# Third softmax's maxima: values' second half first, the queries' last two token tiles after maximum 7

## Chip, cores and metric

The kernel runs on 1 core of one Trainium2 chip. The metric is the device time of one execution in microseconds (us), as the median of several runs.

## What is computed

Input: 16 sequences (batches) of 1024 tokens with 256 channels. Each goes through a Nyström attention block and then through an adapter-gated feed-forward block, each with a LayerNorm before it, a LayerNorm on its output and a residual. Cut to what matters:

```python
def attention(x, w_qkv, w_proj):                   # 16 heads of 16 channels, 64 landmarks
    Q, K, V = split(x @ w_qkv)
    Q_l, K_l = Q.reshape(b, H, M, n // M, HD).mean(-2), K.reshape(b, H, M, n // M, HD).mean(-2)
    kernel1 = softmax(Q @ K_l.T)                   # 1024 x 64 per head
    kernel2 = softmax(Q_l @ K_l.T)                 # 64 x 64
    kernel3 = softmax(Q_l @ K.T)                   # 64 x 1024
    SV = (kernel1 @ iterative_inv(kernel2)) @ (kernel3 @ V)
    return SV @ w_proj

x = x + layernorm(attention(layernorm(x)))
x = x + layernorm(ffn(layernorm(x)))               # base product plus the adapter of the best expert of 8
```

The third softmax (kernel3) needs for each of its rows the maximum of the scores over all 1024 tokens before it can take exponentials.

## The kernel before, in words

The program is written engine by engine: `block.sync` (the DMA queue, SP), `block.gpsimd` (POOL), `block.scalar` (ACT), `block.tensor` (PE) and `block.vector` (DVE) each hold one list of steps per batch, in a function `body(b, more)`. Each engine executes its list strictly in the order in which it is written, and semaphores tie the lists together. The attention of batch b and the feed-forward part of batch b - 1 are interleaved in the same body, so batch 0 has no feed-forward steps, and batches 1 to 15 have them.

**The PSUM ring.** Attention products go through three PSUM banks in turn (`ringA`). The table `USES_A` lists all uses in the order of the TensorE list, and use n has bank n mod 3. `get(b, kind, k)` makes TensorE wait until the use three places earlier has been read. A use of kind `pk` (a token tile of the keys or queries, k from 0 to 7; 0 to 3 keys, 4 to 7 queries) is read twice: ACT copies it as its float16 high part (L634), then DVE subtracts that from it and stores the low part (L1467), and only then is the bank free. A use of kind `pv` (quarter of the value projection, k from 0 to 3) is read once, by ACT (L659). A use of kind `m3` (one product of maxima, k from 0 to 15) is read once, by DVE (L1518).

**The stage around the change.** After the keys, the landmarks and the values' first half come, on TensorE:

- token tiles 4 and 5 (L880), the scores of kernel2 (L972);
- products m3 0 to 3 (L1013), token tile 6, m3 4, token tile 7, m3 5 to 8, values 2, m3 9 to 12, values 3, m3 13 to 15;
- of the feed-forward part of batch b - 1: the channel sums (L1158), then the hidden layer's tile 0 (L1172), the transpose of the folded maxima (L1027), hidden tiles 1 to 3;
- the loop over k of 16: `maxima1` (L1022), `scores3` (L1046), `sum_values` (L1060) and more. `scores3(b, 0)` waits for `fold3`, a DMA.

**ACT** runs in that stage: `staged(2)` (token tiles 4 and 5), `halves2(0)`, `staged(3)` (tiles 6 and 7), `halves2(1)`, `values(2, 3)`. `halves2(g)` (L708) writes the float16 high part of half g of the normalised feed-forward input of batch b - 1. It waits for POOL, which normalises (`norm2`, L534), and POOL then waits for it: `x2lo` (L574) subtracts half g's high part. `staged(3)` also waits for the DMA copies out of the buffer that it overwrites (`stk[1]`).

**SP.** For each pair of token tiles, 12 copies move the staged parts into the stacked operands `KS` and `QS` (L429). Group j = 2 is tiles 4 and 5, group 3 is tiles 6 and 7. In the middle of group 2, after 6 of its 12 copies, stand the two DMA transposes of the feed-forward input (`transposes2`, L399). Each waits for POOL's `x2lo` of its half. After group 2's other 6 copies comes the fold of the third softmax's maxima (L405), which waits for F3T (L673), and then group 3:

```python
for q in range(4):
    if j == 2 and q == 2 and not first(b):
        transposes2(b - 1)
    for a, part in enumerate((0, 1, 0)):
        sp.dma_start(S[32 * a:32 * a + 32, 4 * (j % 2) + q, :],
                     stage[32 * q:32 * q + 32, j % 2, part, :]).then_inc(stk[j].sem, 16)
```

`maxima1(b, 0)` waits for all 12 copies of group 2, and `scores3(b, 0)` for the fold.

Of the kernel before, what the change touches and what calls it, by code (L numbers as in the profile page):

```python
# [40 lines left out]
def sandwich_kernel(nc, x, w_qkv, w_proj, W_base, b_base, Wd1, bd1, Wd2, bd2, Wa_down, ba_down, Wa_up, ba_up, out):  # L41
# [23 lines left out]
    with ctx:  # L65
# [3 lines left out]
        def sig(name, per_batch, unit=1):  # L69
# [102 lines left out]

        USES_A = ([("pk", k) for k in range(4)] + [("kl", 0), ("ql", 0)] + [("pv", k) for k in range(2)]
                  + [("lk", k) for k in range(3)] + [("lq", k) for k in range(2)] + [("pk", k) for k in (4, 5)]
                  + [("m3", k) for k in range(4)] + [("pk", 6), ("m3", 4), ("pk", 7)]
                  + [("m3", k) for k in range(5, 9)] + [("pv", 2)] + [("m3", k) for k in range(9, 13)] + [("pv", 3)]
                  + [("m3", k) for k in range(13, 16)] + [("f3", 0)])
        for k in range(16):
            USES_A += [("m1", k), ("s3", k)]
        USES_A += [("f1", 0)]  # L180
# [429 lines left out]
        def _(act):  # L610
# [17 lines left out]
            def staged(b, js):  # L628
                for j in js:
                    if j >= 2:  # L630
                        act.wait_ge(stk[j - 2].sem, stk[j - 2].at(b, 12))
                    for h in range(2):
                        k = 2 * j + h
                        A(stage[:, j % 2, 0, h * HALF:(h + 1) * HALF], take(b, "pk", k)[:, :], ACT.Copy)\  # L634
                            .then_inc(pk_hi.sem, 1)
# [21 lines left out]
            def values(b, ks):  # L657
                for k in ks:
                    A(V[:, 2 * k:2 * k + 2, :, :], take(b, "pv", k)[:, :].rearrange("p (t a d) -> p t a d", t=2, a=PAIRS),  # L659
                      ACT.Copy).then_inc(freed["pv"].sem, 1)  # L660
# [86 lines left out]
            def body(b, more):  # L747

                ffn = not first(b)
                staged(b, (0, 1))  # L750
                landmarks(b)
                values(b, (0, 1))
                landmark_stack(b)
                staged(b, (2,))
                if ffn:
                    halves2(b - 1, (0,))
                staged(b, (3,))
                if ffn:
                    halves2(b - 1, (1,))
                values(b, (2, 3))  # L760
                if ffn:
                    sums2(b - 1)
                    hidden(b - 1, 0)
                fold_rows3(b)
                kernel2_exp(b)
                if ffn:
                    for t in (1, 2, 3):
                        hidden(b - 1, t)
                for k in range(16):
                    exp3(b, k)  # L770
                    if k == 6:
                        kernel2_transposed(b)
                    if ffn and k in (1, 3, 5, 7):
                        hidden(b - 1, 4 + k // 2)
                fold_rows1(b)
                for k in range(5):
                    ns_copy(b, k)
                    if ffn and k == 4:
                        adapter(b - 1)
                    if first(b) and k == 0:  # L780
                        act.wait_ge(s_setpe.sem, 1)
                        for c in range(KC):
                            A(f_w2T[:, c, :, :], ringF[c][:, :].rearrange("p (q n) -> p q n", q=EP), ACT.Copy).then_inc(s_w2t.sem, 1)
                    if 1 <= k < 4:
                        exp1(b, 2 * k - 2)
                        exp1(b, 2 * k - 1)
                    if k == 3:
                        exp1(b, 6)
                        exp1(b, 7)
                    if more and k < 2:  # L790
                        halves1(b + 1, (k,))
                if ffn:
                    for k in range(4):
                        ffn_out(b - 1, k)
                if first(b):
                    ffn_reduction()
                for k in range(ESLOTS, 2 * ESLOTS):
                    exp1(b, k)
                attn_out(b, (0, 1))
                if more:  # L800
                    pooled(b + 1)
                attn_out(b, (2, 3))
# [18 lines left out]
        def _(pe):  # L821
# [122 lines left out]
            def values(b, ks):  # L944
                for k in ks:
                    ps = get(b, "pv", k)
                    for i in range(2):
                        t = 2 * k + i
                        ins = three(ps[:, i * C:(i + 1) * C], lambda a, kc: xT[:, t, a, kc, :],
                                    lambda a, kc: wqkv[:, a, kc, 2 * C:3 * C])  # L950
                    done(ins, "pv")
# [280 lines left out]
            def body(b, more):  # L1232

                ffn_too = not first(b)
                project(b)
                tokens(b, (4, 5))
                kernel2_scores(b)
                for k in range(4):
                    maxima3(b, k)
                tokens(b, (6,))  # L1240
                for k in range(4, 16):
                    maxima3(b, k)
                    if k == 4:
                        tokens(b, (7,))
                    if k in (8, 12):
                        values(b, (k // 4,))
                if ffn_too:
                    channel_sums(b - 1)
                    hidden(b - 1, 0)
                fold3_transpose(b)  # L1250
                if ffn_too:
                    for t in (1, 2, 3):
                        hidden(b - 1, t)
                for k in range(16):
                    maxima1(b, k)
                    scores3(b, k)
                    if k >= 2:
                        sum_values(b, k - 2)
                    if k == 6:
                        kernel2_transpose(b)  # L1260
                    if ffn_too and k in (1, 3, 5, 7):
                        hidden(b - 1, 4 + k // 2)
                    if k == 10:
                        denominator_rows(b)
                    if k == 12:
                        first_iterate(b)
                for k in range(14, 16):
                    sum_values(b, k)
                if ffn_too:
                    gram(b - 1, 0, range(0, T // 2))  # L1270
                values_transpose(b)
                fold1_transpose(b)
                if ffn_too:
                    gram(b - 1, 0, range(T // 2, T))
                for k in range(5):
                    ns_first(b, k)
                    if first(b):
                        ffn_weights(k)
                    if ffn_too and k < 3:
                        gram(b - 1, k + 1, range(0, T // 2))  # L1280
                    elif ffn_too and k == 3:
                        losses(b - 1)
                    elif ffn_too:
                        adapter(b - 1)
                    if 1 <= k < 4:
                        scores1(b, 2 * k - 2)
                        scores1(b, 2 * k - 1)
                    ns_second(b, k)
                    if k == 3:
                        scores1(b, 6)  # L1290
                        scores1(b, 7)
                        sum_exponentials(b, 0)
                    if ffn_too and k < 3:
                        gram(b - 1, k + 1, range(T // 2, T))
                    if ffn_too and k == 4:
                        ffn(b - 1, 0)
                for i in range(4):
                    thin(b, i, ffn_too and i > 0)
                    if i == 0:
                        sum_exponentials(b, 1)  # L1300
                attend(b, 0)
                for k in range(8, 11):
                    scores1(b, k)
                attend(b, 1)
                for k in range(11, 14):
                    scores1(b, k)
                sum_exponentials(b, 2)
                for k in range(14, 16):
                    scores1(b, k)
                attend(b, 2)  # L1310
                sum_exponentials(b, 3)
                output_projection(b, (0, 1))
                attend(b, 3)
                if more:
                    pool_tokens(b + 1)
                output_projection(b, (2, 3))
# [22 lines left out]
        def _(dve):  # L1339
# [329 lines left out]
            def body(b, more):  # L1669
# [4 lines left out]
                    attn_residual(b - 1)  # L1674
                    statistics(b - 1, 2, xres, x1_done, 4)
                staged(b, (4, 5))
                for k in range(4):
                    maxima3(b, k)
                for k in range(4, 16):
                    maxima3(b, k)  # L1680
                    if k == 4:
                        staged(b, (6, 7))
                fold3_rows(b)
                kernel2_softmax(b)
                if ffn:
# [113 lines left out]
```

## Time and profile before

| | us |
|---|---|
| median of 3 runs | 2277.98 (2277.91 to 2283.66) |
| the profiled execution | 2281.05 |
| its span | 2279.3 |
| PE busy | 2019.9 (89%) |
| DVE busy | 1471.1 (65%) |
| ACT busy | 864.9 (38%) |
| POOL busy | 700.9 (31%) |
| chain that ended last, on PE | 62% of the span |

The span is the time from the first to the last instruction of the profiled execution. Busy time of an engine is the union of its instructions. The chain that ended last is followed back from the last instruction to whatever released each step. In a row of the timeline stand the start in us from the span's start, the length, engine, line, operation, what is written <- what is read, the number of instructions, and in brackets the engine's idle time before the first of them with what ended it.

### The profile page before, as it was taken

The numbers are of one execution on the slowest core, as the hardware profiler recorded it, in microseconds if no ns is written. First come the engines' busy times: TensorE is split into PE (matmuls) and PEld (weight loads), VectorE is DVE, ScalarE is ACT, GpSimd is POOL, SyncE is SP. The second block draws the span as 40 slices with busy tenths as digits, with TensorE's granted clock in tenths as the row PEclk, the third lists the DMA queues.
The fourth block names the chain that finished last, engine by engine and source line by source line (L and its number), as shares of the span: only waits on it lengthen the run. The fifth ranks groups of instructions, "written<-read, shape, count | busy, mean of one in ns | idle before, by whom it ended". The sixth has DMA issues, their size and how long they took to land.

```text
span 2279.3 us, 58742 instructions
## 1 busy us (share of the span) xinstructions
PE 2019.9 (89%) x24991; PEld 1307.2 (57%) x24991; DVE 1471.1 (65%) x3319; ACT 864.9 (38%) x1509; POOL 700.9 (31%) x916
## 2 busy tenths in 40 slices
PE   3888989999898998989899898989989898998945
PEld 1554747556474755647465564746657475665724
DVE  3667576766757667675766757576675757767531
ACT  3334344343433443343343434334343443334320
POOL 4153152322315232232523224251331424223051
PEclk9889999999999999999999999999999999999978
DMA  6213141221514222151422215132231513213020
GB/s 152 46 47 76 30 122 39 81 61 30 121 30 116 44 73 61 29 131 30 112 44 71 66 30 131 30 99 52 63 79 30 129 31 89 62 41 83 11 56 19
DMA packets 232972, 150.71 MB, mean 66 GB/s; under 512 B 153035, under 2 KB 203732, under 8 KB 232693
## 3 DMA queue, kind: packets, MB, share of 16 engines
q1 hardware_dynamic: 232710, 146.95, 27.5%
q8 instruction: 197, 3.23, 0.6%
q14 instruction: 65, 0.53, 0.1%
HBM read 36.98 MB, written 16.78 MB: 24 GB/s over the span
## 4 chain that ended last, share of the span: by engine, by line
PE 62%; DVE 17%; SPq 9%; issue 4%; ACT 3%; POOL 3%; DMA 2%; DVEq 1%; POOLq 0%; ACTq 0%
PE NS L979 11%; PE ringF L1187 9%; SPq L429 9%; PE ringF L1172 6%; PE KV L1060 5%; PE ringA L1146 5%; PE ringA L880 5%; PE ringF L1220 3%; PE ringA L1046 3%; PE ringA L1022 3%; DVE stage L1608 3%; DVE mx L1518 2%; PE ringF L880 2%; PE ringF L1222 2%; ACT E L690 2%
## 5 line engine op out<-in xcount | busy, mean ns | idle before, releaser
L1187 PE MATMUL ringF<-x,H 128*128 128x256 f16 x1536 | 237.9, 273 | 0.0
L1532 DVE TENSOR_REDUCE mx<-ringA 128x8 f32<-128x512 f32 x256 | 175.4, 685 | 89.3 <-PE ringA L1022 88.8
L682 ACT ACTIVATE E<-ringA,score_scale 128x512 f32<-128x512 f32 x256 | 175.5, 686 | 116.8 <-PE ringA L1046 116.7
L1187 PE MATMUL ringF<-H 128*128 128x128 f16 x1024 | 204.4, 220 | 1.4 <-DVE H L1619 1.4
L880 PE MATMUL ringA<-xT,wqkv 128*128 128x512 f16 x768 | 184.0, 391 | 21.2 <-ACT QS L700 11.7
L1585 DVE SCALAR_TENSOR_TENSOR X<-X,NS 128x320 f32<-128x320 f32 x160 | 78.0, 488 | 182.8 <-PE NS L979 177.7
L1518 DVE TENSOR_REDUCE mx<-ringA 128x1 f32<-128x512 f32 x256 | 160.1, 682 | 52.0 <-PE ringA L1013 51.5
L1172 PE MATMUL ringF<-wd,x2T 128*128 128x512 f16 x768 | 187.9, 384 | 6.4 <-DVE H L1619 3.1
L516 POOL TENSOR_SCALAR vtmp<-mv,eps_ffn 128x8 f32<-128x8 f32 x16 | 5.1, 316 | 612.0 <-DVE mv L1363 612.0
L690 ACT ACTIVATE E<-ringA,score_scale 128x512 f32<-128x512 f32 x256 | 158.6, 684 | 75.2 <-PE ringA L1077 75.2
L516 POOL TENSOR_SCALAR vtmp<-mv,eps_ln 128x8 f32<-128x8 f32 x32 | 9.9, 310 | 538.2 <-DVE mv L1363 538.2
L1013 PE MATMUL ringA<-KS,QlB 96*128 96x512 f16 x256 | 100.4, 439 | 67.8 <-DVE stage L1467 55.2
L695 ACT ACTIVATE T<-NS 128x320 f32<-128x320 f32 x160 | 66.3, 437 | 240.0 <-DVE Bc L1578 238.0
L555 POOL TENSOR_TENSOR xin<-xtmp,xin 128x1024 f16<-128x1024 f32 x32 | 71.7, 2241 | 265.7 <-ACT xin L622 265.7
L1467 DVE TENSOR_TENSOR stage<-ringA,stage 128x512 f16<-128x512 f32 x128 | 85.4, 687 | 91.7 <-ACT stage L634 91.2
L880 PEld LDWEIGHTS ringA<-xT,wqkv 128*128 128x128 f16 x768 | 73.2, 100 | 121.0 <-issue 31.7
L1187 PEld LDWEIGHTS ringF<-x,H 128*128 128x128 f16 x1536 | 129.0, 98 | 10.2
L979 PEld LDWEIGHTS NS<-X 64*64 64x64 f32 x3072 | 111.1, 135 | 29.1 <-issue 28.0
L979 PE MATMUL NS<-X 64*64 64x80 f32 (+1 forms) x3072 | 125.5, 230 | 0.6 <-DVE X L1585 0.6
L714 ACT ACTIVATE H<-ringF 128x512 f16<-128x512 f32 x128 | 76.1, 595 | 122.1 <-PE ringF L1172 122.1
L1608 DVE RECIPROCAL stage<-KV 128x256 f32<-128x256 f32 x64 | 107.7, 1724 | 22.3 <-PE KV L1116 22.3
L880 PE MATMUL ringA<-wqkv,xT 128*128 128x256 f16 x768 | 109.1, 304 | 14.5 <-DVE stage L1467 11.4
(261 smaller groups left out, 4317.8 us busy)
## 6 DMA issues: line engine op xcount, KB each, us to landing
KS<-stage SPq DMA_DIRECT2D x384, 64.0 KB, 2.0
QS<-stage SPq DMA_DIRECT2D x384, 64.0 KB, 2.0
xin<-in_L_attn_x_dram SPq DMA_DIRECT2D x16, 1024.0 KB, 11.0
xres<-in_L_attn_x_dram SPq DMA_DIRECT2D x16, 1024.0 KB, 8.1
out_dram<-yout SPq DMA_DIRECT2D x16, 1024.0 KB, 5.5
QS<-LB SPq DMA_DIRECT2D x16, 512.0 KB, 4.4
E<-in_L_attn_w_qkv_dram SPq DMA_DIRECT2D x1, 768.0 KB, 7.0
H<-in_L_ffn_Wd_dram SPq DMA_DIRECT2D x2, 256.0 KB
```

Of the source, the lines that this page charges most:

```text
L429: sp.dma_start(S[32 * a:32 * a + 32, 4 * (j % 2) + q, :], stage[32 * q:32 * q + 32, j % 2, part, :]).then_inc(stk[j].sem, 16)
L682: A(E[:, k % ESLOTS, :], ps[:, :], ACT.Exp, scale=score_scale[:, 0:1]).then_inc(freed["s3"].sem, 1)
L690: A(E[:, k % ESLOTS, :], ps[:, :], ACT.Exp, scale=score_scale[:, 0:1]).then_inc(freed["s1"].sem, 1)
L880: ins = MM(dst, left(a, k), right(c, k), start=n == 0, stop=n == 3 * KC - 1)
L979: ins = MM(dst[r, :], left[r, p, :], right(r, e, p), start=True, stop=True)
L1060: ins = MM(KV[32 * j:32 * j + 32, (2 * g + i) * P:(2 * g + i + 1) * P], onesf[:, :] if i else V[:, t, p, :], E[:, k % ESLOTS, j * P:(j + 1 ...
L1146: ins = MM(ps[:, i * C:(i + 1) * C], svT[:, kc, t * P:(t + 1) * P], wproj[:, kc, :], start=kc == 0, stop=kc == KC - 1)
L1172: ins = MM(ps[:, :], x2T[:, t, a, kc, :], wd1[:, c, kc, :], start=n == 0, stop=n == 5)
L1187: ins = MM(dst, H[:, a, t, own], src, start=first and i == 0, stop=last and i >= 3, skip_group_check=True)
L1518: V_.reduce_max(mx3[:, k // 2, k % 2:k % 2 + 1], take(b, "m3", k)[:, :], AX.X).then_inc(freed["m3"].sem, 1)
L1532: V_.reduce_max(mx1[:, t, 8 * h:8 * h + 8], take(b, "m1", k)[:, :].rearrange("p (a m) -> p a m", a=8), AX.X)\
L1608: ins = V_.reciprocal(svT[:, i % 2, cols], bank("ss", i)[:, part * HALF // 2:(part + 1) * HALF // 2])
```

## The change

Three lists and the table of PSUM uses are rewritten in another order. No instruction is added or removed. On TensorE, values 2 come after m3 3, values 3 and token tile 6 after m3 7, token tile 7 after m3 9. On ACT, the evictions of values 2 and 3 come before `halves2(0)`. On DVE, the low part of tile 6 comes after maximum 7 and that of tile 7 after maximum 9. SP's and POOL's lists stay as they are.

```diff
@@ the table of PSUM uses @@
-                  + [("m3", k) for k in range(4)] + [("pk", 6), ("m3", 4), ("pk", 7)]
-                  + [("m3", k) for k in range(5, 9)] + [("pv", 2)] + [("m3", k) for k in range(9, 13)] + [("pv", 3)]
-                  + [("m3", k) for k in range(13, 16)] + [("f3", 0)])
+                  + [("m3", k) for k in range(4)] + [("pv", 2)] + [("m3", k) for k in range(4, 8)] + [("pv", 3), ("pk", 6)]
+                  + [("m3", 8), ("m3", 9), ("pk", 7)] + [("m3", k) for k in range(10, 16)] + [("f3", 0)])
@@ ACT @@
                 staged(b, (2,))
+                values(b, (2, 3))
                 if ffn:
                     halves2(b - 1, (0,))
                 staged(b, (3,))
                 if ffn:
                     halves2(b - 1, (1,))
-                values(b, (2, 3))
@@ PE @@
-                for k in range(4):
+                for k in range(16):
                     maxima3(b, k)
-                tokens(b, (6,))
-                for k in range(4, 16):
-                    maxima3(b, k)
-                    if k == 4:
-                        tokens(b, (7,))
-                    if k in (8, 12):
-                        values(b, (k // 4,))
+                    if k in (3, 7):
+                        values(b, (k // 4 + 2,))
+                    if k in (7, 9):
+                        tokens(b, (k // 2 + 3,))
@@ DVE @@
-                for k in range(4):
+                for k in range(16):
+                    if k in (8, 10):
+                        staged(b, (k // 2 + 2,))
                     maxima3(b, k)
-                for k in range(4, 16):
-                    maxima3(b, k)
-                    if k == 4:
-                        staged(b, (6, 7))
```

On TensorE, in the second batch (the same in each later one), between the scores of kernel2 and the channel sums. Before:

```order
L972 MATMUL NS<-KlC,QlB 128x64 x8
L1013 MATMUL ringA<-KS,QlB 128x512 x4
L880 MATMUL ringA<-xT,wqkv 128x512 x6
L1013 MATMUL ringA<-KS,QlB 128x512
L880 MATMUL ringA<-xT,wqkv 128x512 x6
L1013 MATMUL ringA<-KS,QlB 128x512 x4
L880 MATMUL ringA<-wqkv,xT 128x256 x12
L1013 MATMUL ringA<-KS,QlB 128x512 x4
L880 MATMUL ringA<-wqkv,xT 128x256 x12
L1013 MATMUL ringA<-KS,QlB 128x512 x3
L1158 MATMUL ringF<-ones,x 128x1 x32
```

With the change (lines are one lower there):

```order
L971 MATMUL NS<-KlC,QlB 128x64 x8
L1012 MATMUL ringA<-KS,QlB 128x512 x4
L879 MATMUL ringA<-wqkv,xT 128x256 x12
L1012 MATMUL ringA<-KS,QlB 128x512 x4
L879 MATMUL ringA<-wqkv,xT 128x256 x12
L879 MATMUL ringA<-xT,wqkv 128x512 x6
L1012 MATMUL ringA<-KS,QlB 128x512 x2
L879 MATMUL ringA<-xT,wqkv 128x512 x6
L1012 MATMUL ringA<-KS,QlB 128x512 x6
L1157 MATMUL ringF<-ones,x 128x1 x32
```

The rows of 12 are the values' quarters, the rows of 6 the token tiles. The values now stand between the first two groups of four maxima products, and the token tiles behind the eighth and the tenth.

On ACT, in the second batch, from token tiles 4 and 5 on. Before:

```order
L634 ACTIVATE stage<-ringA 128x512 x2
L708 ACTIVATE x<-yout 128x4x256
L634 ACTIVATE stage<-ringA 128x512 x2
L708 ACTIVATE x<-yout 128x4x256
L659 ACTIVATE V<-ringA 128x512 x2
L711 ACTIVATE xsum<-ringF 128x2
```

With the change:

```order
L633 ACTIVATE stage<-ringA 128x512 x2
L658 ACTIVATE V<-ringA 128x512 x2
L707 ACTIVATE x<-yout 128x4x256
L633 ACTIVATE stage<-ringA 128x512 x2
L707 ACTIVATE x<-yout 128x4x256
L710 ACTIVATE xsum<-ringF 128x2
```

Both `halves2` (x<-yout) now stand behind the values' evictions; the second one stands, as before, behind token tile 7.

## Rows read from the trace of the kernel before

**Rows 1.** The page, part 1: busy time of each engine.
```profile
PE 2019.9 (89%) x24991; PEld 1307.2 (57%) x24991; DVE 1471.1 (65%) x3319; ACT 864.9 (38%) x1509; POOL 700.9 (31%) x916
```
**Rows 2.** Waits of PE: who waited for whom: total us, times, longest.
```profile
PE ringA L1013 <- DVE stage L1467: 55.2, 48, 3.8
```
**Rows 3.** Timeline, batch 7, from m3 0 to the loop.
```profile
988.26 0.38 PE L1013 MATMUL ringA<-KS,QlB 96*128 96x512 f16 x1
989.59 2.48 DVE L1518 TENSOR_REDUCE mx<-ringA 128x1 f32<-128x512 f32 x4
990.93 1.47 PE L880 MATMUL ringA<-xT,wqkv 128*128 128x512 f16 x6 [0.21 <-DVE mx L1518]
...
994.20 1.06 ACT L708 ACTIVATE x<-yout 128x1024 f16<-128x1024 f32 x1 [5.38 <-POOL yout L534]
995.25 1.08 ACT L634 ACTIVATE stage<-ringA 128x512 f16<-128x512 f32 x2
995.88 1.29 DVE L1467 TENSOR_TENSOR stage<-ringA,stage 128x512 f16<-128x512 f32 x2 [2.54 <-ACT stage L634]
996.22 4.20 POOL L574 TENSOR_TENSOR x<-yout,x 128x1024 f16<-128x1024 f32 x2
996.34 1.06 ACT L708 ACTIVATE x<-yout 128x1024 f16<-128x1024 f32 x1
...
996.63 0.98 PE L1013 MATMUL ringA<-KS,QlB 96*128 96x512 f16 x3 [2.72 <-DVE stage L1467]
...
998.42 2.72 PE L880 MATMUL ringA<-wqkv,xT 128*128 128x256 f16 x12
...
1002.74 1.48 PE L880 MATMUL ringA<-wqkv,xT 128*128 128x256 f16 x12 [0.21 <-DVE mx L1518]
...
1004.26 0.60 ACT L659 ACTIVATE V<-ringA 128x512 f32<-128x512 f32 x1 [2.49 <-PE ringA L880]
...
1005.14 0.94 PE L1158 MATMUL ringF<-ones,x 128*128 128x1 f16 x32
...
1012.06 0.39 PE L1046 MATMUL ringA<-QlB,KS 112*128 112x128 f16 x4
```
**Rows 4.** Timeline, batch 7, the DMA queue of SP.
```profile
998.43 4.51 SPq L399 DMA_TRANSPOSE x2T<-x  x2
1002.99 5.00 SPq L429 DMA_DIRECT2D QS<-stage  x6
1008.28 0.65 SPq L405 DMA_DIRECT2D QlB<-F3T  x1
1009.06 7.74 SPq L429 DMA_DIRECT2D QS<-stage  x12
```
**Rows 5.** DMA transposes x2T<-x by source line: ns min/median/max of the issue.
```profile
L399 SPq DMA_TRANSPOSE x2T<-x x32: 1582/2209/4054, 192.0 to 2207.4; - x32
```
**Rows 6.** The page, part 6: issues, KB each, median us to landing.
```profile
QS<-stage SPq DMA_DIRECT2D x384, 64.0 KB, 2.0
...
QlB<-F3T SPq DMA_DIRECT2D x16, 32.0 KB, 2.1
```
**Rows 7.** Windows, batch 7: length, busy PE, PEld, DVE, ACT, POOL (instructions), PEclk, DMA.
```profile
996.60:998.40 1.80, 1.47 (x4) 0.31 (x4) 1.80 (x4) 0.80 (x1) 1.80 (x2) 0.77 0.45 109
998.40:1001.20 2.80, 2.80 (x15) 1.91 (x14) 1.16 (x2) 0.02 (x1) 2.01 (x1) 0.54 0.71 141
1002.70:1005.00 2.30, 2.00 (x15) 1.38 (x16) 1.70 (x3) 0.60 (x1) 0.00 (x0) 1.00 1.11 206
```
**Rows 8.** Timeline of PE: m3 0 and scores3 0 in batches 8 and 9.
```profile
1122.06 0.38 PE L1013 MATMUL ringA<-KS,QlB 96*128 96x512 f16 x1
...
1147.21 0.39 PE L1046 MATMUL ringA<-QlB,KS 112*128 112x128 f16 x4
...
1257.22 0.39 PE L1013 MATMUL ringA<-KS,QlB 96*128 96x512 f16 x1
...
1280.04 0.39 PE L1046 MATMUL ringA<-QlB,KS 112*128 112x128 f16 x4
```

## The prediction

> **What bounds the kernel now.** I read the busy times first: TensorE is at work for 89% of the span, and the other engines for 65% or less [rows 1]. So a change is worth what it does to the time in which TensorE stands still or runs slowly. Then I read the waits of PE: L1013, the maxima products, waited 55.2 us for DVE's low parts of the token tiles, the longest time 3.8 us [rows 2]. Then the timeline of one batch shows which wait that is [rows 3]. Times from here on are us after the start of m3 0 (988.26) in batch 7. Token tile 6 starts at 2.67, m3 4 and token tile 7 follow, and then m3 5 has to wait for the low part of tile 6. That comes late because ACT stands at `halves2(0)`: its input from POOL arrives at 5.94, it takes 1.06, and only then does ACT evict tile 6 (6.99). PE is idle for 2.72 and restarts at 8.37.
>
> The idle time has a follower. The granted clock is 1.00 ahead of it, then 0.77 and 0.54 in the next two windows, and 1.00 again from 1002.70 on [rows 7]. 0.5 is the lower level (1.2 GHz). The 12 matmuls of values 2 fall there and take 2.72; the same 12 of values 3 take 1.48 at the full level [rows 3]. So the wait costs 2.7, and the clock behind it 1.24.
>
> The stage ends for TensorE when the loop begins with `scores3(b, 0)`, at 23.80 in this batch. In batch 8 that is 25.15 and in batch 9 22.82 after m3 0 [rows 8]. The mean of the three is 23.92. From there on the loop's PE work is the same before and after, so I price the change by where this instruction goes.
>
> **What the change does on TensorE, ACT and DVE.** Values 2 take the place of tile 6 and start at 2.67; at full clock they end at 4.15. m3 4 and 5 follow, and their maxima end near 5.1 and 5.7 (the four of the first row take 2.48, 0.62 each). Values 3 need the bank of m3 5 and run from 5.74 to 7.2; ACT evicts them until 7.85 (0.60). Tile 6 is then already running. The 2.72 of idle time and the low clock behind values 2 are gone: worth up to 2.7 + 1.24 = 3.9 per batch on TensorE, if nothing later holds it.
>
> But ACT's order has a price. `halves2(0)` was at 5.94 to 7.00; it now stands behind values 3 and runs from 7.9 to 8.95. Tile 6's high part follows (0.5 to 0.6), its low part ends near 10.2 (0.05 + 0.69), and tile 7, which has the same bank, can start only at 10.25. It ends at 11.75, its high part at 12.4, and `halves2(1)` comes after it, to 13.45. Before, tiles 6 and 7 were evicted back to back and `halves2(1)` began at 8.08. POOL's subtraction of the second half takes 2.10 (half of 4.20) and ended at 12.16; it was POOL's own work that set it. Now it waits for ACT and ends at 13.5 + 2.10 = 15.6, **3.4 later**. TensorE has its own idle stretches left: about 0.8 before tile 7, and 0.8 before m3 12, which needs the low part of tile 7 (near 13.0). The last maximum comes near 16.6, where DVE has 3 more to do after m3 12.
>
> **Where it goes from there: SP's queue.** On SP the second DMA transpose waits for that subtraction, and behind it in the same list stand 6 copies of group 2 and then the fold, for which `scores3(b, 0)` waits. Before, the transposes started at 10.17 and 12.26, the 6 copies ended at 19.73, and the fold was issued at 20.02, when F3T was there, and landed 2.1 later, at 22.1 [rows 4, 6]. `scores3` came at 23.80: this path had 1.7 to spare, and TensorE, busy with the channel sums and hidden tiles, set the start.
>
> Now: from the end of the subtraction (12.16) to the end of the 6 copies it took 7.57 before. That is one end. The other end: the transposes are further apart now (near 11.2 and 15.7), so one issue may take 1.9 where the two took 4.51 together (the shortest of all is 1.58, the median 2.21) [rows 4, 5], and 6 copies at the pace of the next twelve (7.74 / 12 = 0.645) take 3.9: 6.0 with the small steps between. So SP is free at 21.6 to 23.2, the fold lands 2.1 later, at 23.7 to 25.3, and `scores3(b, 0)` follows at once. The middle is 24.5 for batch 7. In batches 8 and 9 ACT and PE start a little later or at another clock, and the same sum applies. Against the mean of 23.92 this is **+0.6 per batch**, with ends at -0.2 and +1.4.
>
> TensorE's own work would be ready earlier: the channel sums start once the subtraction is done (15.65), and from L1158 to `scores3` it took 6.92 [rows 3], so 22.6. So 1.9 of waiting stands ahead of the loop where none was before, about 1 ahead of `maxima1` (the copies land last at 23 to 24) and the rest ahead of `scores3`.
>
> **The clock in the loop.** The trace has one wait of this size before, 2.72, and a low clock behind it [rows 3, 7]. None of 1.0 plus 0.9 with a little work between is shown. Bounds: nothing, or 1.24 per batch as for values 2 [rows 3]. I take a third of it, 0.4, since the wait is shorter and broken in two. The Trainium skill ("TensorE: Matmul & The Clock Gate", section "HAM oscillation — how this bites in real kernels") counts the penalty as half of the throttled time. Here the granted clock lost 1.8 x 0.23 + 2.8 x 0.46 = 1.7 in the two windows. By that rule the upper bound would be 1.7 per batch, and the sum below 0.15 x 15 = 2 us more; the rows show 1.24 on the 12 matmuls, and part of the low stretch fell elsewhere.
>
> **The sum.** Batches 1 to 15 have the feed-forward steps: (0.6 + 0.4) x 15 = 15 us. Batch 0 has no `halves2` and no `transposes2`; its TensorE may gain about 1, which I leave in the range. SP's group 3 (12 copies, 7.74) starts some 3 later, ends near 31, and is needed by maximum 8 of the loop, near 38: nothing. POOL ends 3.4 later and next has the first normalisation of the next batch, whose statistics come in the middle of the loop: nothing. The profiled execution took 2281.05, 3 us or 0.13% above the median of 2277.98, so I put the 15 on the median: **2293 us**. About 0.3% (7 us) is what a measurement of this kernel can tell from no change, 0.46 per batch.
>
> **Rivals.**
> - *TensorE keeps its gain, faster.* If the fold has landed when TensorE arrives, `scores3` comes at 22.6, 1.3 earlier than the mean of before: -1.3 x 15 = -20, 2258 us. For it: the idle time of 2.72 does vanish. Against: SP would have to be free by 20.5, which even with the shortest issue times needs the second subtraction at 14.5, more than 1 earlier than my sum of ACT's, DVE's and PE's steps. Chance 0.13.
> - *The fold's path ends where it did, same.* The low end of SP's range (-0.2) up to +0.4 with no low clock: -3 to +6, near 2280 us. For it: an isolated transpose may be issued in 1.6 to 1.9. Chance 0.26.
> - *My forecast, slower*: +0.5 to +1.8 per batch, 2285 to 2305, about 2293 us. Chance 0.48.
> - *The wait ahead of the loop brings the low clock in every batch.* SP's path at its upper end (+1.4) and 1.24 to 1.7 of clock: +2.6 to +3.1, 2317 to 2324 us. For it: the same thing happens at m3 5 before. Against: the wait is shorter. Chance 0.13.
>
> **How the numbers follow.** Slower is 0.48 + 0.13 = 0.61, same 0.26, faster 0.13. The range leaves out the outer part of the first rival and of the last, one tenth each: 2266 to 2314.
>
> **What would show it.** Right: L1013's wait for the low parts shrinks to less than 1.5 per batch and no longer has a low clock behind it; values 2 take 1.5; POOL's second L574 ends near 15.6 after m3 0; SP no longer waits for F3T, the fold is issued at 21.6 to 23.2, and PE's `maxima1` and `scores3` now wait for DMA in each batch, 1 to 2 in all. `scores3(b, 0)` stands at 24 to 25. Wrong: the fold still waits for F3T, or there is no DMA wait ahead of the loop; then the first rival holds. A low clock inside the loop in most batches points to the last. It would also be wrong if the early idle time stays, because values 2 or 3 wait for something that I took as ready.

## The result: 0.66% slower, with two limits that lie close together

The changed kernel takes 2289.98 us (median of 7 runs, 2286.14 to 2297.61), the kernel before 2277.91 us (7 runs). The ratio is 1.0066, with an interval of 1.0043 to 1.0089. The profiled execution of the changed kernel took 2297.61 us, the slowest of the seven, so its trace shows some 8 us more than the median has. The granted clock over the seven runs goes from 0.963 (2286.14) to 0.956 (2297.61), the slower the lower.

Busy time, on the page of the changed kernel, part 1:

```profile
PE 2035.6 (89%) x24991; PEld 1310.5 (57%) x24991; DVE 1471.3 (64%) x3319; ACT 863.8 (38%) x1509; POOL 705.1 (31%) x916
```

The instructions are the same, but TensorE is busy for 15.7 us more than before [rows 1]. The same matmuls take longer, so it is the clock: the stretches at its lower level add up to 202 us, before to 168. The waits of PE (who waited for whom, total us, times, longest):

```profile
PE ringA L1012 <- DVE stage L1463: 30.1, 48, 1.0
PE ringA L879 <- DVE stage L1463: 29.2, 32, 1.1
...
PE ringA L1012 <- DVE mx L1514: 13.1, 63, 0.2
...
PE ringA L1045 <- DMA QlB<-F3T: 4.7, 6, 2.8
...
PE ringA L1021 <- DMA QS<-stage: 1.7, 3, 0.9
```

The products' wait for the low parts has fallen from 55.2 us (longest 3.8) [rows 2] to 30.1 (longest 1.0): the long wait ahead of m3 5 is gone. In its place stand two waits of about 1: token tile 7 waits for the low part of tile 6, and m3 12 for that of tile 7. Waits for DMA ahead of the loop (L1021 and L1045 are `maxima1` and `scores3`) are few. Batch 4 of the changed kernel, in order of time; its m3 0 starts at 585.61:

```profile
585.61 0.38 PE L1012 MATMUL ringA<-KS,QlB 96*128 96x512 f16 x1
...
588.34 1.48 PE L879 MATMUL ringA<-wqkv,xT 128*128 128x256 f16 x12 [0.21 <-DVE mx L1514]
...
593.44 1.05 ACT L707 ACTIVATE x<-yout 128x1024 f16<-128x1024 f32 x1
...
595.01 0.69 DVE L1463 TENSOR_TENSOR stage<-ringA,stage 128x512 f16<-128x512 f32 x1 [2.44 <-ACT stage L633]
...
595.75 1.47 PE L879 MATMUL ringA<-xT,wqkv 128*128 128x512 f16 x6 [1.12 <-DVE stage L1463]
...
597.75 1.05 ACT L707 ACTIVATE x<-yout 128x1024 f16<-128x1024 f32 x1
...
598.64 0.39 PE L1012 MATMUL ringA<-KS,QlB 96*128 96x512 f16 x1 [0.98 <-DVE stage L1463]
598.98 2.12 POOL L573 TENSOR_TENSOR x<-yout,x 128x1024 f16<-128x1024 f32 x1 [2.19 <-ACT x L707]
599.24 0.39 PE L1012 MATMUL ringA<-KS,QlB 96*128 96x512 f16 x1 [0.21 <-DVE mx L1514]
...
601.20 0.99 PE L1157 MATMUL ringF<-ones,x 128*128 128x1 f16 x32 [0.38 <-issue]
...
602.05 2.72 PE L1171 MATMUL ringF<-wd,x2T 128*128 128x512 f16 x6
...
604.91 5.62 PE L1171 MATMUL ringF<-wd,x2T 128*128 128x512 f16 x18
...
610.38 0.39 PE L1021 MATMUL ringA<-KlB,QS 96*128 96x128 f16 x4
...
610.60 0.39 PE L1045 MATMUL ringA<-QlB,KS 112*128 112x128 f16 x4
```

In this batch values 2 take 1.48, at full clock; before they took 2.72 [rows 3]. In 8 of the 15 batches with feed-forward steps (3, 5, 6, 7, 9, 12, 14, 15) they are slow again, 2.12 to 2.74. Batch 5, its m3 0 at 720.79:

```profile
723.57 2.67 PE L879 MATMUL ringA<-wqkv,xT 128*128 128x256 f16 x12 [0.21 <-DVE mx L1514]
```

The granted clock is 0.50 there from 723.7 to 727.1, with no long wait ahead of it, only one of 0.60 and three of 0.21 between m3 0 and values 2; batch 4 has the same waits to within 0.04 and keeps the full clock. Those 8 batches reach `scores3` at 26.1 on average, the other 7 at 24.9.

In batch 4 the second half's high part is written at 12.1 (before 8.1) and POOL's second subtraction ends at 15.5 (before 12.2). SP's queue in the same batch:

```profile
596.88 6.03 SPq L398 DMA_TRANSPOSE x2T<-x  x2
602.96 4.39 SPq L428 DMA_DIRECT2D QS<-stage  x6
607.47 0.65 SPq L404 DMA_DIRECT2D QlB<-F3T  x1
```

The fold is issued at 21.9 after m3 0, where it was 20.0 [rows 4]. Yet `scores3` at 610.60 does not wait for it. It landed at 24.0, and TensorE arrived at 25.0. The windows of this batch (length, busy PE, PEld, DVE, ACT, POOL, PEclk, DMA share, GB/s) say why:

```profile
597.60:600.90 3.30, 1.61 (x5) 0.38 (x4) 3.01 (x6) 1.20 (x2) 1.92 (x1) 0.98 0.84 159
600.90:607.60 6.70, 6.40 (x46) 2.72 (x47) 3.93 (x10) 1.53 (x4) 0.20 (x1) 0.50 0.62 126
607.60:610.60 3.00, 2.93 (x17) 1.22 (x16) 1.38 (x2) 1.22 (x3) 0.00 (x0) 1.00 0.36 80
```

In the last maxima products TensorE is busy for 1.61 of 3.30: one wait of 0.98, then one of 0.21 ahead of each product, for DVE's maxima. After that the granted clock is 0.50 (1.2 GHz) for the channel sums and the hidden tiles: tile 0 takes 2.72. So it is, for the whole of tile 0 or a part of it, in 14 of the 15 batches. Batch 11 had no low clock there, and shows the other limit (timeline of PE, m3 0 at 1535.3):

```profile
1552.02 1.46 PE L1171 MATMUL ringF<-wd,x2T 128*128 128x512 f16 x6
...
1558.82 0.40 PE L1021 MATMUL ringA<-KlB,QS 96*128 96x128 f16 x4 [0.91 <-DMA QS<-stage]
1559.68 0.40 PE L1045 MATMUL ringA<-QlB,KS 112*128 112x128 f16 x4 [0.47 <-DMA QlB<-F3T]
```

So there are two candidates for where the early gain went: **the fold** (SP's queue is late) and **the clock** (TensorE is slow in the hidden tiles). On average over batches 1 to 15, from the start of m3 0 to that of `scores3(b, 0)`, it is 24.2 before and 25.5 now; from there to the next m3 0 it is 110.1 and 109.9. The difference of 1.3 x 15 = 19 us, less some 3 us elsewhere, is the difference of the two profiled spans (16.6). Two means split the 1.3. The channel sums start at 17.3 before and at 16.4 now, 0.9 earlier; from there to `scores3` it takes 6.9 before and 9.1 now, 2.2 longer. Nor did the idle time go away: between m3 0 and `scores3` TensorE stood still for 4.9 per batch before and does so for 5.0 now.

### The profile page after: what moved, and what is told of

Its sections match the earlier page's. It is cut to its first block, busy times and chain, and to the rows that moved or that the text cites. A ratio compares the mean times of both kernels' runs of the same rounds, so it can differ in the third digit from the quotient of the medians.

```text
span 2295.9 us, 58742 instructions
## 1 busy us (share of the span) xinstructions
PE 2035.6 (89%) x24991; PEld 1310.5 (57%) x24991; DVE 1471.3 (64%) x3319; ACT 863.8 (38%) x1509; POOL 705.1 (31%) x916
## 4 chain that ended last, share of the span: by engine, by line
PE 62%; DVE 18%; POOL 6%; ACT 4%; issue 4%; SPq 3%; DMA 2%; DVEq 1%; POOLq 0%; ACTq 0%
PE NS L978 11%; PE ringF L1186 9%; PE ringF L1171 7%; PE KV L1059 5%; PE ringA L1145 5%; PE ringA L879 4%; PE ringF L1219 3%; POOL QS L533 3%; PE ringA L1045 3%; PE ringA L1021 3%; DVE stage L1604 3%; DVE mx L1514 3%; DVE stats L1353 2%; SPq L428 2%; PE ringF L879 2%
## 5 line engine op out<-in xcount | busy, mean ns | idle before, releaser
L1171 PE MATMUL ringF<-wd,x2T 128*128 128x512 f16 x768 | 215.8, 428 | 4.4 <-DMA x2T<-x 2.9
L879 PE MATMUL ringA<-xT,wqkv 128*128 128x512 f16 x768 | 178.9, 383 | 35.6 <-DVE stage L1463 17.8
L1615 DVE SCALAR_TENSOR_TENSOR H<-ringF,H 128x512 f16<-128x512 f32 x128 | 87.8, 686 | 75.2 <-ACT H L713 75.2
L1012 PE MATMUL ringA<-KS,QlB 96*128 96x512 f16 x256 | 94.5, 409 | 46.2 <-DVE stage L1463 30.1
L1171 PEld LDWEIGHTS ringF<-wd,x2T 128*128 128x128 f16 x768 | 72.8, 106 | 108.7 <-issue 42.8
L1186 PEld LDWEIGHTS ringF<-x,H 128*128 128x128 f16 x1536 | 129.0, 98 | 10.2
```

Of the source, the lines that this page charges most:

```text
L879: ins = MM(dst, left(a, k), right(c, k), start=n == 0, stop=n == 3 * KC - 1)
L1012: done(MM(ps[:, :], QlB[0:96, p, :], KS[0:96, p, h * HALF:(h + 1) * HALF], start=True, stop=True), "m3")
L1171: ins = MM(ps[:, :], x2T[:, t, a, kc, :], wd1[:, c, kc, :], start=n == 0, stop=n == 5)
L1186: ins = MM(dst, H[:, a, t, own], src, start=first and i == 0, stop=last and i >= 3, skip_group_check=True)
L1615: V_.scalar_tensor_tensor(out=H[:, 1, t, :], in0=bank("h", t)[:, :], scalar=0.0, in1=H[:, 0, t, :], op0=ALU.max, op1=ALU.subtract).then_in ...
```

## The experiments

Theory A: the late fold holds the loop. Theory B: TensorE's own chain holds it, with its low clock. A third, formed after the first four runs: the two lie so close together that removing one uncovers the other.

In the table, times are means over batches 1 to 15 after m3 0 in the profiled execution; the last column is the sum of the low-clock stretches (us) in its whole trace. The profiled execution is not the median one: it lies 8 us above the median for the changed kernel and 4 for e4, and 7 us below it for e10, 5 for e6 and 4 for e2. So the columns of the trace tell where time goes, and the ratios what a kernel is worth. Ratios are against the kernel before, run beside each.

| kernel | median us | ratio (interval) | 2nd subtraction ends | fold lands | scores3 0 | low clock |
|---|---|---|---|---|---|---|
| before | 2277.91 | | 12.2 | 22.7 | 24.2 | 168 |
| changed | 2289.98 | 1.0066 (1.0043, 1.0089) | 16.3 | 25.0 | 25.5 | 202 |
| e1 halves early | 2270.47 | 0.9977 (0.9968, 0.9987) | 13.6 | 22.8 | 23.9 | 157 |
| e2 transposes later | 2290.99 | 1.0074 (1.0056, 1.0092) | 15.9 | 22.9 | 24.9 | 175 |
| e6 extra matmuls | 2277.34 | 1.0004 (0.9991, 1.0017) | 15.7 | 24.3 | 24.4 | 115 |
| e4 tile 6 first | 2272.49 | 0.9986 (0.9972, 1.0000) | 12.3 | 22.2 | 24.1 | 171 |
| e7 = e1 + extra | 2256.83 | 0.9917 (0.9903, 0.9932) | 13.5 | 22.6 | 23.0 | 119 |
| e8 = e2 + extra | 2257.95 | 0.9938 (0.9920, 0.9956) | 15.6 | 22.4 | 23.0 | 99 |
| e9 = before + extra | 2262.07 | 0.9946 (0.9932, 0.9960) | 12.3 | 22.0 | 23.3 | 99 |
| e10 = e4 + extra | 2259.69 | 0.9931 (0.9918, 0.9944) | 12.2 | 21.5 | 22.9 | 104 |
| e5 transposes first | 2312.94 | 1.0160 (1.0146, 1.0174) | 15.7 | 26.3 | 26.4 | 195 |
| e11 = e5 + extra | 2331.98 | 1.0226 (1.0209, 1.0243) | 16.1 | 26.7 | 26.8 | 192 |
| e13 = e1 + e2 + extra | 2269.21 | 0.9959 (0.9945, 0.9972) | 13.7 | 21.8 | 23.6 | 130 |

**e1: the second half between tiles 6 and 7, on ACT.**

```diff
                 if ffn:
                     halves2(b - 1, (0,))
-                staged(b, (3,))
+                staged_one(b, 6)
                 if ffn:
                     halves2(b - 1, (1,))
+                staged_one(b, 7)
```

> The changed kernel, with the high part of the feed-forward input's second half written on ACT between token tiles 6 and 7 instead of behind tile 7. Times after the start of m3 0 of a batch. Both theories: POOL's second subtraction ends near 13.3 instead of 15.5 to 17.2, SP is free near 20, and the fold lands near 22.3 instead of 24 to 26. Theory A (SP's queue, the late fold, holds the loop): scores3 0 moves with it from 25.5 (mean of batches 1 to 15) to 22.3 to 22.8, about -2.9 per batch, near 2247 us, 1.3% under the kernel before. Theory B (TensorE's own chain holds it, because its clock is low in the hidden tiles after thin work in m3 10 to 15): the low clock stays, channel sums start at 15.2, scores3 0 at 23.7 to 24.5, about -1.4 per batch, near 2269 us, 0.4% under the kernel before.

The fold landed at 22.8, and `scores3` came at 23.9, 1.1 behind it: B's number. The low clock stood in the hidden tiles in 14 of 15 batches; in the one without it `scores3` came at 22.2.

**e2: three instead of six copies between the transposes and the fold, on SP.**

```diff
-                        if j == 2 and q == 2 and not first(b):
+                        if j == 2 and q == 3 and not first(b):
```

> The changed kernel, with SP's two transposes of the feed-forward input behind 9 instead of 6 of group 2's copies, so that only 3 copies stand between them and the fold. Fold issued near 19.7 and landed near 21.8 after m3 0 instead of 24 to 26 (some later where tile 6 is late). ACT, DVE and PE untouched, so the low clock stays. Theory A: scores3 0 moves from 25.5 to 22.8, -2.7 per batch, near 2249 us. Theory B: only the waits for DMA that the changed kernel shows ahead of maxima1 and scores3 in five batches go (0.4 to 1.4 each), -0.2 to -0.4 per batch, near 2285 us, 0.3% over the kernel before.

The fold was 2.1 earlier and the time did not move (1.0074 against 1.0066). A is refuted as the only reason: with the fold out of the way TensorE still arrives at 24.9. B had 2285 here, 6 us less than measured; the waits for DMA that it took away were worth nothing that the medians show.

**e6: something to do in the thin stretch.**

```diff
+            def filler(b):
+                ps = get(b - 1, "xs", 0)
+                for n in range(FILL):                # FILL = 5
+                    MM(ps[:, :], wqkv[:, 0, 0, 0:P], xT[:, 0:4, 0, 0, :], start=True, stop=True)
...
+                    if ffn_too and k == 11:
+                        filler(b)
```

> The changed kernel, with 5 extra float16 matmuls of 512 columns behind m3 11, into the bank that the channel sums overwrite afterwards; they only keep TensorE at work where it waits 1.0 for the low part of tile 7. They cost 0.1 to 0.3 per batch by themselves, and leave ACT, POOL and SP where they are. Theory A: nothing changes at the loop, the fold still lands at 24 to 26: 2290 us plus up to 4. Theory B: if the low clock in the hidden tiles goes, TensorE's own chain is ready at 22.7 to 24, DMA waits of 1 to 2 appear ahead of the loop in nearly all batches, and scores3 0 comes right behind the fold's landing, at 24.0 to 25.8: -0.5 per batch, 2282 us. If the fill doesn't bring the clock up, 2290 to 2294 and the point stays open.

The extra matmuls fill the wait of 0.98, and the following m3 products start when they did. Waits of PE in this run:

```profile
PE ringA L1022 <- DMA QS<-stage: 9.8, 10, 1.2
...
PE ringA L1046 <- DMA QlB<-F3T: 7.9, 13, 2.7
```

The loop now waits for DMA in most batches, and `scores3` stands 0.05 behind the landing of the fold on average. The hidden tiles are at the low clock in 5 of 15 batches instead of 14, and values 2 in 2 instead of 8. With that, the whole kernel is back at the time of before (1.0004). So the low clock carried about 0.6%, in both places together. The late fold by itself costs almost nothing against the kernel before, because it lands (24.3) where `scores3` stood anyway (24.2).

**e4: a version with both ends kept.** TensorE: tile 6 right behind m3 7, values 3 behind m3 9, then tile 7, with the table of uses in that order.

```diff
                 staged(b, (2,))
-                values(b, (2, 3))
+                values(b, (2,))
                 if ffn:
                     halves2(b - 1, (0,))
-                staged(b, (3,))
+                staged_one(b, 6)
                 if ffn:
                     halves2(b - 1, (1,))
+                values(b, (3,))
+                staged_one(b, 7)
```

> A version meant to keep both ends: values 2 behind m3 3 as in the changed kernel, but tile 6 right behind m3 7, values 3 behind m3 9 and then tile 7; ACT evicts values 2, then first half, tile 6, second half, values 3, tile 7. The halves are then written as early as in the kernel before (5.9 and 8.0), POOL's second subtraction ends at 12.2, SP's fold is issued near 19.8. Early idle time of 2.7 does not return. Theory A: scores3 0 near 22.3, -1.9 per batch against the kernel before (24.2), near 2249 us. Theory B: the same if the clock stays up; if the work in m3 10 to 15 is still thin and the clock falls in the hidden tiles, 23.7 to 24.2, 2271 to 2278 us.

POOL and SP are as early as before and the early wait stays away, yet no gain is clear of the noise (0.14%, with an interval that ends at 1.0000): the low clock moved from values 2 to the hidden tiles, where it stands in all 15 batches.

**e7, e8, e10: both limits at once.** Each adds the same `filler` at the same place.

> Both limits of the changed kernel taken away at once: the second half's high part written between tiles 6 and 7 (fold lands at 22.8 instead of 25.0 after m3 0) and the 5 extra matmuls behind m3 11 (no low clock in the hidden tiles). Two limits that lie together (the theory after the first four runs): each alone gave 0.6 to 1.6 per batch, together scores3 0 comes right behind the fold, near 22.6, 1.6 earlier than in the kernel before (24.2) and 2.9 earlier than in the changed one: 2250 to 2256 us. Theory B alone (the clock is all of it, the fold was never a limit): the extra matmuls gave 0.8 per batch in the changed kernel and would give no more than that here, near 2260. Theory A alone: 2270, as without the extra matmuls.

> The changed kernel with SP's transposes behind 9 copies (fold lands at 22.9) and the 5 extra matmuls. Transposes later alone gave nothing (2291 us), the extra matmuls alone 2277 us. Two limits that lie together: channel sums still start at 15.6 (they wait for POOL), scores3 0 at 22.6 to 23.2, near 2257 to 2263 us. Theory B alone: 2277 us, as with the extra matmuls alone.

> The version with tile 6 right behind m3 7 and values 3 behind m3 9, which had its fold at 22.2 but the low clock in the hidden tiles and 2272 us, with the 5 extra matmuls behind m3 11. Two limits: scores3 0 at 22.2 to 22.5, 1.8 per batch under the kernel before, near 2249 us. If the clock stays low: 2272 us.

e8 decides: putting the transposes later gains nothing alone (2291), the extra matmuls alone bring 2277, both 2258, within the range of two limits and 19 us below that of the clock alone. e7 says less. Its 2257 lies between the two forecasts (2250 to 2256, and 2260). e10 missed: it came 11 us later than I expected, and 7 of 15 batches still had the clock low, in a profiled execution that was the fastest of its five. e7 gains 0.83% against the kernel before, e10 0.69% and e8 0.62%; all three beat the two kernels that were compared.

**e9: the clock behind the old wait.** In the kernel before, 12 extra matmuls behind tile 7.

> The kernel before, with 12 extra matmuls of 512 columns in its 2.7 wait ahead of m3 5, into the bank that the channel sums overwrite later. It measures what the low clock behind that wait costs by itself. If the clock stays up: values 2 take 1.5 instead of 2.7, scores3 0 comes at 22.8 instead of 24.2, 1.4 per batch, near 2255 us. If the clock there cost nothing (DVE's maxima or ACT's evictions hide it): 2276 us plus up to 3.

Timeline of PE in batch 7 of this run (m3 0 at 979.8):

```profile
985.78 2.75 PE L1154 MATMUL ringF<-xT,wqkv 128*128 128x512 f16 x12
988.37 0.86 PE L1014 MATMUL ringA<-KS,QlB 96*128 96x512 f16 x3
...
990.13 1.48 PE L881 MATMUL ringA<-wqkv,xT 128*128 128x256 f16 x12
```

The wait is as long as before, only filled, and values 2 take 1.48. On average over batches 1 to 15 they took 2.52 before and take 1.53 now, 0.99 less. `scores3` moves by as much, 0.96 (24.2 to 23.3), and the kernel gains 0.54%. So what the low clock takes there reaches the loop nearly whole.

This number also bounds what the new order itself is worth. The kernel before, with nothing but its wait filled, stands at 0.9946 (0.9932 to 0.9960). The rearranged and filled kernels e8 (0.9938) and e10 (0.9931) are not clear of that; e7 (0.9917) is better by about 0.3%. Most of the gain of these kernels comes from the extra matmuls.

**e5, e11: the fold later still.** `q == 1` in place of `q == 2` on SP, without and with the extra matmuls.

> The other direction: the changed kernel with SP's transposes behind only 3 of group 2's copies, so that 9 copies (5.7) instead of 6 (3.8) stand between them and the fold. ACT, DVE, PE untouched. The fold lands 1.9 later, near 26.9 after m3 0 instead of 25.0. Two limits that lie together: the mean slack of the fold ahead of scores3 0 is 0.5, so scores3 0 moves from 25.5 to about 27.0, +1.4 per batch, 2311 us. If the fold were no limit at all (clock alone): 2290 us.

> The same 9 copies behind the transposes, and the 5 extra matmuls, with which the fold was the limit in every batch (scores3 0 came 0.05 behind its landing, 2277 us). Two limits: the whole 1.9 shows, scores3 0 near 26.3 instead of 24.4, 2277 + 1.9 x 15 = 2305 us, near the kernel without the extra matmuls, since the fold holds both. Waits for DMA ahead of the loop in all batches. If they bring a low clock into the loop, 5 to 20 us more.

e5 has `scores3` 0.05 behind the fold, as forecast, and its 2313 us lie beside the 2311. But in part that is luck: fold and `scores3` came 0.6 earlier than forecast (26.3 and 26.4), and a low clock in the loop, which was not in the forecast, made it up. It stands in 6 of 15 batches, and the time from `scores3(b, 0)` to the next m3 0 is 1.6 longer in them (111.2 against 109.6). e11 should have been no slower (2305, and 5 to 20 us more with a low clock in the loop), and was, by 19 us; it lies 7 us above the upper end. With the hidden tiles at full clock TensorE arrives early, and the wait ahead of the loop grows. Its row among the waits of e11 (in e5 this row has 16.1, 14 times):

```profile
PE ringA L1022 <- DMA QS<-stage: 41.8, 15, 3.6
```

And the windows around it, in batch 4:

```profile
614.30:617.10 2.80, 0.02 (x1) 0.02 (x2) 0.00 (x0) 0.60 (x1) 0.00 (x0) 1.00 0.39 95
617.10:620.50 3.40, 3.19 (x20) 2.10 (x21) 2.60 (x5) 1.38 (x2) 0.00 (x0) 0.50 0.47 105
```

The low clock now falls into the loop, in 14 of 15 batches: from `scores3(b, 0)` to the next m3 0 it is 111.36 on average, 1.4 more than in the changed kernel (109.93).

**e13: the fold out of the way on both sides.**

> The fold's path shortened on both sides (second half written between tiles 6 and 7, and 9 copies ahead of the transposes) and the 5 extra matmuls. The fold lands near 21 to 21.5 and waits for nothing but F3T, so TensorE's own chain is alone: 22.2 to 22.3 in batches without a low clock, 23.4 with one. Against the run with early halves and extra matmuls (23.0 on average, of which 0.4 behind the fold) at most -0.3 per batch: 2252 to 2257 us. If it equals that run, the fold is no longer a limit.

It was 12 us above e7, where at most equal was expected. A third limit came up: with 9 copies ahead of them, the transposes are issued later, and hidden tile 0 waits for them. Batch 3, TensorE, then the waits of the whole run:

```profile
461.37 0.94 PE L1170 MATMUL ringF<-ones,x 128*128 128x1 f16 x32
463.71 1.62 PE L1184 MATMUL ringF<-wd,x2T 128*128 128x512 f16 x6 [1.39 <-DMA x2T<-x]
```

```profile
PE ringF L1184 <- DMA x2T<-x: 8.6, 9, 1.7
```

Of these 8.6 us, 7.1 in 8 of the batches 1 to 15 are new against e7, which has such a wait once (1.5). Behind the wait the clock is low once more (the granted clock was 0.50 from 464.90 to 468.30). With the second half written early, six copies behind the transposes are the better place.

## Why the prediction was right, and where it was not

- **The time and the sign were right**: 2293 forecast, 2290 measured, ratio 1.0066 where 1.0066 was forecast (2293 / 2278). That they agree so closely is luck: the seven runs spread over 11 us, and the sum was made of the wrong parts, as follows.
- **The early wait**: right. The 2.72 of idle time is gone, and the waits for low parts are 1.1 and 0.98 where 0.8 and 0.8 were forecast. **Its clock**: right in 7 of 15 batches only. In the other 8 values 2 are slow without the wait, 2.04 on average over all 15 where 1.5 was forecast.
- **The price on ACT, POOL and SP**: right nearly to the tenth where the clock stayed up. In batch 4 the steps came at (forecast in brackets) 7.8 (7.9) for `halves2(0)`, 10.1 (10.2) for the low part of tile 6, 15.5 (15.6) for the end of the second subtraction, 21.9 (21.6 to 23.2) for the issue of the fold. Over batches 1 to 15 the subtraction ends at 16.3 on average, up to 17.3 where values 2 were slow. SP stopped waiting for F3T: before it did so in 13 of these batches, now in none.
- **The term that failed** is "TensorE's own work would be ready earlier: ... from L1158 to `scores3` it took 6.92, so 22.6". In batch 4 it took 610.60 - 601.20 = 9.4. The 6.92 came from a batch whose clock was at the full level there. I had written down the two idle pieces before tile 7 and before m3 12, but not asked what they do to the clock behind them; I put the low clock in the loop instead, behind a wait for DMA that mostly did not come. The changed kernel waits for DMA ahead of the loop for 4.7 + 1.7 = 6.4 us in all, 2.8 of them in batch 0 and the rest in 5 of the other 15 (3, 7, 10, 11, 12), not 1 to 2 in each. `scores3` stands at 25.5 on average, not at 24 to 25. By the sign named beforehand, no wait for DMA ahead of the loop would have meant the first rival; ten batches have none, and that rival did not hold, because TensorE's own work came later.
- **So the sum was right with wrong shares.** I had 0.6 per batch for the fold and 0.4 for the clock. By the ratios the change costs 15 us, 1.0 per batch. With the clock mostly up and the fold as it is (e6) 0.04% is left, under 0.1 per batch. With the clock as it is and the fold out of the way (e2) nothing comes back. So the slowdown is the clock's, behind m3 10 to 15 and at values 2; the late fold decides only what is left to gain once the clock is up (e6 against e8, 0.66%). The mean of three batches for the kernel before, 23.9, was also 0.3 below that of all 15. The price of a low clock in the loop, 1.24 to 1.7, was right (1.6 in e5 and 1.7 in e11 between batches with and without it; in e11 one batch alone is without), but the changed kernel has none there.
- **The rivals.** "TensorE keeps its gain" needs the fold early and the clock up: e7, e8 and e10 come near that case, 2257 to 2260 where 2258 was worked out, with `scores3` at 22.9 to 23.0 instead of 22.6. It did not need the second subtraction at 14.5: in e8 that ends at 15.6. The last rival, a low clock in the loop in every batch, is seen only with a fold that is later than in the rival's sum: e11, 2332 against 2317 to 2324.

What stays open: why the clock falls in some batches and not in others that do the same work (batch 11 of the changed kernel, batch 1 of e1; values 2 in 8 of 15 batches of the changed kernel, in 3 of e2). Whether the number of slow values 2 sets the spread between runs is not shown, since one trace per kernel is kept.

## What to carry to other kernels

A wait that is removed at one place can come back as a thin stretch at another, and here the clock was low behind thin stretches too, not only behind long waits. Count the idle time of the whole stage before and after, and look at the clock in every batch, not in one. When a list of one engine is reordered, follow each of its outputs over POOL and the DMA queue to the instruction that needs it last, and look how close the second limit lies behind the first: here the fold's three copies alone gave nothing and the extra matmuls alone 0.6%, both together 1.3% (1.0066 to 0.9938). A few matmuls without a use, in a bank that is overwritten later, are a cheap test of whether a stretch suffers from the clock. Try them on the kernel before, too: there they gave most of what the new order and they gave together (0.54% of 0.62 to 0.83%).

## What was new about the hardware

- The granted clock fell to 0.50 behind a stretch in which TensorE was busy for 1.61 of 3.30 us, with no wait longer than 0.98. The Trainium skill describes such a case ("TensorE: Matmul & The Clock Gate", section "A second HAM failure mode: psum-queue depth-cycling"): many short idle pieces between groups of matmuls can lower the clock too. The traces here agree: five more matmuls in the 0.98 brought the low stretches of the whole trace from 202 to 115 us (e6).
- With the clock low the hidden tile's six matmuls took 2.72 instead of 1.46. Behind an idle wait of 2.7, the low clock cost the twelve matmuls of values 2 0.99 per batch on average, and the start of the loop 0.96 (before against e9).
- On the DMA queue of SP, what stands ahead of an issue in the list sets when it starts: six copies of 64 KB took 3.67 from the first issue to the end of the last, 0.61 each, and three copies less between transposes and fold moved the fold's landing by 2.1 us (e2).
